# Attention with two chains of exponentiated scores: who adds the softmax denominators' parts, and five score banks in the last block

## The reference

```
x = x + attention(q = layernorm(x), kv = ctx)       # 16 heads of 32, 3202 keys, mask: key <= query
x = x + ffn(layernorm(x))                           # a mixture of 8 experts between two projections

scores = (q @ Wq.T + bq) . (kv @ Wk.T + bk) * 32**-0.5
attn   = softmax(where(key <= query, scores, -inf))
out    = (attn . (kv @ Wv.T + bv)) @ Wo.T + bo
```

## Time and profile before

| | us |
|---|---|
| median of three runs | 2900.06 |
| profiled execution, its own time | 2903.43 |
| its span, first to last instruction | 2901.8 |
| attention, about | 268 to 2051 |
| TensorE busy, share of the span | 2803.8, 97% |
| VectorE | 1873.2, 65% |
| GpSimd | 1570.4, 54% |
| ScalarE | 1521.4, 52% |

### The profile page before, as it was taken

One profiled execution on the slowest core, in us unless ns is written; L12 is line 12 of the kernel. 1 busy time (PEld: TensorE's weight loads), 2 busy tenths in 40 slices (PEclk: granted clock), 3 DMA queues, 4 the chain that ended last, 5 costly groups with the idle time before them and its releaser, 6 DMA issues. The chain is left out here.

```text
span 2901.8 us, 42115 instructions
## 1 busy us (share of the span) xinstructions
PE 2803.8 (97%) x15464; PEld 1655.4 (57%) x15464; DVE 1873.2 (65%) x3483; ACT 1521.4 (52%) x2904; POOL 1570.4 (54%) x717
## 2 busy tenths in 40 slices
PE   8989999999999999999999999999889999999996
PEld 7877555555555555555554555553576666655653
DVE  4367888886688876778876788860663544344544
ACT  3232456666566667566666566666334343444332
POOL 0000377888678888677888678888661210111110
PEclk9998899999999999999999999999999999999998
DMA  6568456668746778756778656677693110011000
GB/s 243 188 195 245 127 143 152 152 154 186 176 134 157 160 161 190 182 138 153 159 162 193 161 146 139 146 165 193 194 315 117 44 34 26 30 44 44 30 29 15
DMA packets 138708, 407.89 MB, mean 141 GB/s; under 512 B 11632, under 2 KB 28528, under 8 KB 111888
## 3 DMA queue, kind: packets, MB, share of 16 engines
q0 software_dynamic: 32272, 226.77, 33.2%
q1 hardware_dynamic: 101056, 169.07, 20.3%
q10 hardware_dynamic: 5184, 9.44, 1.0%
HBM read 114.33 MB, written 70.78 MB: 64 GB/s over the span
## 5 line engine op out<-in xcount | busy, mean ns | idle before, releaser
L1063 DVE TENSOR_REDUCE row_max<-m_bank 128x1 f32<-128x512 f32 (+4 forms) x2240 | 1254.1, 624 | 269.1 <-PE m_bank L1168 171.5
L1046 ACT ACTIVATE pT<-s_bank 128x512 f32<-128x512 f32 (+5 forms) x2176 | 1085.6, 578 | 621.6 <-PE s_bank L1213 444.6
L986 POOL TENSOR_TENSOR part_sum<-part_sum,pT 128x2048 f32<-128x2048 f32 (+1 forms) x252 | 1032.7, 4098 | 159.0 <-ACT pT L1046 150.8
L1213 PE MATMUL s_bank<-q_sb,k_sb 104*128 104x512 f32 (+3 forms) x2176 | 841.0, 411 | 12.6 <-ACT pT L1046 7.5
L1168 PE MATMUL m_bank<-k_sb,q_sb 96*128 96x512 f32 (+4 forms) x2240 | 843.9, 410 | 8.7 <-DVE den L1090 3.1
L1168 PEld LDWEIGHTS m_bank<-k_sb,q_sb 96*128 96x128 f32 x2240 | 432.3, 196 | 209.3 <-DVE row_max L1063 127.2
L1213 PEld LDWEIGHTS s_bank<-q_sb,k_sb 104*128 104x128 f32 x2176 | 411.5, 192 | 215.4 <-ACT pT L1046 124.4
L1230 PE MATMUL o_bank<-pT,v_sb 128*32 128x512 f32 (+5 forms) x4352 | 497.3, 574 | 0.0
L1639 POOL TENSOR_TENSOR f_var_eps<-f_mean_var,eps 128x4 f32<-128x4 f32 x8 | 1.6, 202 | 474.0 <-DVE f_mean_var L1858 474.0
L1230 PEld LDWEIGHTS o_bank<-pT,v_sb 128*32 128x32 f32 (+1 forms) x4352 | 113.3, 109 | 229.2 <-ACT pT L1046 112.2
L986 POOL TENSOR_TENSOR part_sum<-pT 128x2048 f32<-128x2048 f32 x28 | 127.8, 4565 | 134.9 <-ACT pT L1046 134.9
(11 more groups left out here) (198 smaller groups left out, 3378.4 us busy)
## 6 DMA issues: line engine op xcount, KB each, us to landing
moved_sum<-pT POOLq DMA_DIRECT2D x208, 1024.0 KB, 7.3
q_sb<-qT_hi SPq DMA_DIRECT2D x64, 256.0 KB, 5.1
k_sb<-kT_hi SPq DMA_DIRECT2D x48, 256.0 KB, 9.5
x_in<-in_x SPq DMA_DIRECT2D x8, 1024.0 KB, 6.1
qT_hi<-q_hi SPq DMA_DIRECT2D x8, 1024.0 KB, 4.2
qT_lo<-q_lo SPq DMA_DIRECT2D x8, 1024.0 KB, 6.5
q_sb<-qT_lo SPq DMA_DIRECT2D x32, 256.0 KB, 4.7
aT<-o_sb ACTq DMA_DIRECT2D x32, 256.0 KB, 5.3
```

Of the source, the lines that this page charges most:

```text
L986: pool.tensor_tensor(total, pT[:, slot(S - 1), :, q0:] if j and kt == 1 else total, pT[:, slot(S), :, q0:], ALU.add).then_inc(pool_added, 1)
L1046: act.activation(pT[0:rows, slot(S), h, q0:], s_bank[(HG * S + h) % S_RING][0:rows, q0:], ACT.Exp, scale=SCALE).then_inc(exp_done, 1)
L1063: dve.tensor_reduce(row_max[:, j % 2, r, h, c:c + 1], m_bank[p % M_BANKS][:, 0:n], AX_X, ALU.max).then_inc(unit_max, 1)
L1213: mm = pe.matmul(out[:, q0:], k_sb[0:R_END, h, at:at + P], q_sb[query_buffer(g, j)][0:R_END, h, q0:], start=True, stop=kt < 4 * j)
```

## The change

It has four parts.

1. In blocks 1 to 6 of each group, VectorE adds both chains into GpSimd's part (`fold`, two additions of 128 x 2048 values, float32, both inputs in SBUF). It does so one step into the next block (`FOLD_AFTER` = 1), behind the maxima of that step. TensorE then sums `part_sum` alone. There are 24 such blocks, so 48 additions.
2. The denominators of these blocks stand four steps into the next block in place of two (`DEN_AFTER`). The first moves of the next block's chains wait for the fold in place of the denominators.
3. In the last block five banks hold scores in place of three, two of `m_bank` joining the ring.
4. In the last block VectorE adds from key tile 4 on in place of 18 (`LAST_ADDS`). `STORE` goes from 7 to 6.

The planner learns of these: a fold costs VectorE 2.35 us in its list, the denominators cost TensorE less, and the last block's scores wait for a bank five back. So the whole order of units changes with it.

```diff
-LAST_ADDS = 18
+LAST_ADDS = 4
...
-DEN_AFTER, INVERT, SPREAD, NORMALISE, STORE = 2, 1, 2, 3, 7
-SUMS_BEHIND = {ST * g + FIRST_STEP[j + 1] + DEN_AFTER: (g, j) for g in range(NG) for j in range(QB) if (g, j) != (NG - 1, QB - 1)}
+DEN_AFTER, INVERT, SPREAD, NORMALISE, STORE = 4, 1, 2, 3, 6
+SUMS_BEHIND = {ST * g + FIRST_STEP[j + 1] + (DEN_AFTER if 0 < j < QB - 1 else 2): (g, j)
+               for g in range(NG) for j in range(QB) if (g, j) != (NG - 1, QB - 1)}
+FOLD_AFTER = 1
+def folded_chains(g, j):
+    if j in (0, QB - 1):
+        return ()
+    return range(CHAINS) if j >= 1 else range(1)
...
+T_FOLD = 2.35
+LAST_SCORE = HG * (len(ALL_STEPS) - key_tiles(QB - 1))
+def score_before(n):
+    if n < LAST_SCORE + S_RING:
+        return n - S_RING
+    return n - LAST_RING if n >= LAST_SCORE + LAST_RING else None
...
+        if h == HG - 1 and S in FOLDS_AT:
+            x = x._replace(dve=max(x.dve, end) + T_FOLD * len(folded_chains(*FOLDS_AT[S])))
...
-                        reach(pool, block_done, QB * g + (j if j > 1 else 0))
+                        if (*previous_chains(g, j), c) in FOLD_NUMBER:
+                            reach(pool, folded, FOLD_NUMBER[(*previous_chains(g, j), c)])
+                        else:
+                            reach(pool, block_done, QB * g + (j if j > 1 else 0))
...
+                def fold(g, j):
+                    reach(dve, pool_added, PO * g + PO_BEFORE[FIRST_STEP[j + 1]])
+                    for c in folded_chains(g, j):
+                        reach(dve, moved[c], 16 * (TR[c] * g + TR_BEFORE[c][FIRST_STEP[j + 1]]))
+                        reach(dve, folded, FOLD_NUMBER[g, j, c] - 1)
+                        dve.tensor_tensor(part_sum[:, j % 2], part_sum[:, j % 2], moved_sum[:, c], ALU.add).then_inc(folded, 1)
...
-                    for c in range(CHAINS) if j else ():
+                    chains = [c for c in range(CHAINS) if j and c not in folded_chains(g, j)]
+                    for c in chains:
...
+                    if folded_chains(g, j):
+                        reach(pe, folded, FOLD_NUMBER[g, j, folded_chains(g, j)[-1]])
...
-                    out = s_bank[n % S_RING]
+                    out = score_bank(n)
```

More of the change, by code:

```diff
@@ L456 @@
 S_RING, M_BANKS = 3, 4
+LAST_RING = S_RING + 2
 def key_tiles(j):
@@ L536, with previous_chains @@
 TR = [TR_BEFORE[c][ST] for c in range(CHAINS)]
-DEN_AFTER, INVERT, SPREAD, NORMALISE, STORE = 2, 1, 2, 3, 7
-SUMS_BEHIND = {ST * g + FIRST_STEP[j + 1] + DEN_AFTER: (g, j) for g in range(NG) for j in range(QB) if (g, j) != (NG - 1, QB - 1)}
+DEN_AFTER, INVERT, SPREAD, NORMALISE, STORE = 4, 1, 2, 3, 6
[6 more added lines that the diff above has]
+    return range(CHAINS) if j >= 1 else range(1)
+FOLDS = [(g, j, c) for g in range(NG) for j in range(QB) for c in folded_chains(g, j)]
+FOLD_NUMBER = {fold: n + 1 for n, fold in enumerate(FOLDS)}
+FOLDS_AT = {ST * g + FIRST_STEP[j + 1] + FOLD_AFTER: (g, j) for g, j, _ in FOLDS}
+def previous_chains(g, j):
+    return (g, j - 1) if j > 1 else (g - 1, QB - 1)
 def max_units(j):
@@ L670, in sums_time @@
             return 0
-        j = SUMS_BEHIND[2 * v][1]
+        g, j = SUMS_BEHIND[2 * v]
         own = sum(widths(j, kt) for kt in range(key_tiles(j)) if adder(j, kt) == "matmul")
-        return T_VALUES * (1 + (CHAINS if j else 0) + own) + T_TURN
+        return T_VALUES * (1 + (CHAINS - len(folded_chains(g, j)) if j else 0) + own) + T_TURN
     def slot_free(self, x, S):
@@ L704, in score @@
         turn, behind = self.turned(x)
-        pe = max(x.pe, x.exp_end[0] + T_TO_WRITE) + turn + self.score_time(j, kt)
+        before = score_before(x.n)
+        pe = max(x.pe, x.exp_end[before - x.n] + T_TO_WRITE if before is not None else 0) + turn + self.score_time(j, kt)
         act = max(x.act, pe + T_TO_READ) + 0.06 + (T_EXP - 0.06) * widths(j, kt)
         end, copied = act + T_EXP_END - T_EXP, x.copied
+        if h == HG - 1 and S in FOLDS_AT:
+            x = x._replace(dve=max(x.dve, end) + T_FOLD * len(folded_chains(*FOLDS_AT[S])))
         if x.n + 1 == x.copied_by:
@@ L756, in best @@
     def best(self):
-        kept = [State(0, 0, 0, "scores", 9, 0, 0, 0, (0,) * S_RING, (), (0,) * M_BANKS, 0, 0, 0, None)]
+        kept = [State(0, 0, 0, "scores", 9, 0, 0, 0, (0,) * LAST_RING, (), (0,) * M_BANKS, 0, 0, 0, None)]
         for _ in range(self.scores + self.pairs + len(self.left)):
@@ L862, in attend @@
         p_used = t.sem("p_used")
+        folded = t.sem("chains_folded")
         pool_added, moved = t.sem("pool_added"), [t.sem(f"moved_sum_added{c}") for c in range(CHAINS)]
@@ L866, in attend, with score_bank @@
         TILES = HG * ST
+        def score_bank(n):
+            if n < LAST_SCORE:
+                return s_bank[n % S_RING]
+            k = (n - LAST_SCORE) % LAST_RING
+            return s_bank[(LAST_SCORE + k) % S_RING] if k < S_RING else m_bank[(len(BANK_JOBS) - S_RING + k) % M_BANKS]
         def slot(S):
@@ L1045, in _ @@
                         reach(act, s_done, HG * S + h + 1)
-                        act.activation(pT[0:rows, slot(S), h, q0:], s_bank[(HG * S + h) % S_RING][0:rows, q0:],
+                        act.activation(pT[0:rows, slot(S), h, q0:], score_bank(HG * S + h)[0:rows, q0:],
                                        ACT.Exp, scale=SCALE).then_inc(exp_done, 1)
@@ L1122, in _ @@
                         spread(*SUMS_AT[S - SPREAD])
+                    if S in FOLDS_AT:
+                        fold(*FOLDS_AT[S])
                     if vector_adds(g, j, kt):
@@ L1209, in scores @@
                     n = HG * S + h
-                    reach(pe, exp_done, max(0, n - S_RING + 1))
-                    out = s_bank[n % S_RING]
+                    before = score_before(n)
+                    if before is None:
+                        bank_free(len(BANK_JOBS) - S_RING + n - LAST_SCORE)
+                    else:
+                        reach(pe, exp_done, max(0, before + 1))
+                    out = score_bank(n)
                     at = key_column(g, kt)
```

4 lines of the change are left out of this document (2 added, 2 removed).

## The result

| | median, us | runs, us | profiled span, us | mean clock |
|---|---|---|---|---|
| before | 2901.4 | 4: 2897.0 to 2902.9 | 2901.8 | 0.979 |
| after | 2981.2 | 4: 2977.3 to 2997.2 | 2977.9 | 0.965 |

The ratio is 1.028, with an interval of 1.026 to 1.030: slower by 80 us. The forecast was 2915, its range ended at 2938. The sign was right, the size was not.

A forecast was written before the change was run, and what follows sets the result against it. TensorE was taken to set attention's pace, with VectorE also near its limit. The terms - 26 - 5 + 52 - 5 + 9 - 10 = +15 us on a median of 2900.1 gave 2915 us, range 2872 to 2938.

The forecast's parts named there:

- chains' matmuls gone, sparse pairs, piles: In attention: TensorE's saved matmuls with ones, -26 and -5 us; fewer step pairs without units, -5; piled units in group 0, +9.
- TensorE waits for the folds: At the denominators of blocks 1 to 5: 46 us of waits plus 6 where four units stand ahead, 52 us in all.
- last block: Moves leave earlier, with the DMA as the next limit: gain 10 us, bounds 18 and 4.
- So the two engines take turns: VectorE's folds and GpSimd's 4.57 us addition, both reading SBUF, exclude each other for a whole instruction; folds end at 901.3.
- The step that failed: At the denominators behind the folds: TensorE can do nothing else and waits 2.3 us, 20 times, 46 us.
- Its own upper bound: For the folds: VectorE's whole 3.5 us of waiting and part of its 4.6 us of work on TensorE's path, 100 us.
- The third rival: In dense blocks VectorE becomes the bound, maxima, folds and waiting together exceeding TensorE's work: 2945 us; chance 0.14.
- The piles: In group 0, units pushed to the step where they fall due, 23, 22 and 18 in three pairs: cost 9 us.
- Pairs of 5.2 us: In the last block each pair of steps brings a 1.05 MB move, so pairs go from 5.5 to 5.2 us.
- The first rival: VectorE's folds are not held by GpSimd and the 52 us go: 2863, up to 2880 where half are held; chance 0.30.

The follow-up runs named there:

- run 9: The changed kernel with folds that add only 8 of each tile's 512 queries, the order of every engine kept: 2880.2 us, ratio 0.993.
- run 5: The changed kernel with ten useless matmuls ahead of TensorE's wait, only at the 11 places where it waits for the fold alone: 2963.2 us, ratio 1.021.
- run 3: The changed kernel with GpSimd's first addition of blocks 2 to 7 done over 8 of 512 queries, the folds whole: 2879.8 us, ratio 0.9915.
- run 7: The changed kernel with one chain folded, at step 0 of the next block where GpSimd is idle, and denominators at 2 steps: 2877.9 us, ratio 0.991.
- run 1: The changed kernel with only its last block's part: no folds, denominators two steps behind in every block: 2895.8 us, ratio 0.9975.
- run 2: The changed kernel with the last block's three score banks and VectorE's additions from key tile 18 restored, folds kept: 2991.2 us, ratio 1.031.

## Why the prediction was right in sign and wrong in size

The account on the profiled executions, 76 us (2977.9 - 2901.8). A block's time is that between two copies of its output on ScalarE. Two terms are read from the traces as they are, the waits and the last block. The clock is half of a count of low clock, and the first row is not measured: it is what the other three leave of 76.

| term | predicted | found |
|---|---|---|
| chains' matmuls gone, sparse pairs, piles: -31 - 5 + 9 | -27 | -24 (the rest) |
| TensorE waits for the folds | +52 | +61 |
| last block | -10 | -10 |
| TensorE's clock | none | +49 (half of 99 us) |
| sum | +15 | +76 |

*The folds.* "So the two engines take turns" held at 4.57 us as at 1.3, which no row of before showed. Moved to the new place (GpSimd's start there is 37.9 us later), the prediction had GpSimd done at 935.0, the folds at 939.2 and TensorE ready at 936.9; the trace has 935.0, 939.5 and 937.1. The Trainium skill's "SBUF — State Buffer", section "SBUF: two separate sides", has the port pair held for the whole instruction; run 9's 0.19 us addition that takes 4.47 us agrees. The term itself was too small by 9: the 20 waits of blocks 1 to 5 came to 56 us (about 2.5 each, 3.06 where a fourth unit stands ahead), and blocks 6 of groups 0 to 2, which I costed at nothing, waited 2.47, 1.23 and 1.12 us.

*The step that failed* is "TensorE waits 2.3 us. 20 times that is 46 us": a wait was priced at its own length. The prediction noted the upper clock level ahead of the change and had no term for it behind. In the blocks behind block 0 of group 0 the clock was low for 105.5 us in the changed kernel and for 17 in the one before; in the 100 us behind attention for 17 and 6.8. Half of the difference is 49 us (the later stages, with 47 and 44, are left out). Of the 105.5, 72 stand behind 13 of the 23 waits, so 61 us of waiting cost about 36 more; 20 stand behind the two large piles. That low clock costs about half its length can be read where the same block ran with and without it. Block 1 of group 1, which neither fold nor pile touches, in the kernels before, after, and of run 9:

```profile
768.31:799.34 31.03, 29.62 (x196) 16.26 (x194) 20.78 (x44) 15.90 (x35) 18.55 (x8) 0.89 0.36 112
```
```profile
802.75:832.12 29.37, 28.40 (x194) 15.34 (x193) 19.62 (x42) 15.71 (x34) 18.35 (x8) 0.94 0.40 123
```
```profile
777.10:804.84 27.74, 26.75 (x194) 14.79 (x193) 19.60 (x42) 15.61 (x34) 18.33 (x8) 1.00 0.50 143
```

31.0 us with 6.8 us of low clock, 29.4 with 3.4, 27.7 with none: 0.48 us for each. So the kernel before was itself slowed there by a fall, and a difference of one block between two kernels need not come from its code. Run 5's blocks gave 0.4; at that price the clock's term is 39 and the first row -14. By half, runs 3 and 9, which have no such waits, leave -29 and -26 in the first row, near the change's -24. Undoing the turns (run 3) took away 61 us of waits and 67 of low clock in the blocks (38 are left of 105.5), 34 at half: 95 of the 101 us. The prediction's term for the folds was 52. Its own upper bound was 100, and the range had left that out: 2915 + 48 = 2963 should have been its end. The third rival's own 2945 lay outside it too. Even 2963 is 18 us short.

*The third rival* (VectorE becomes the bound) falls as the account of the 101 us. In run 3 VectorE does all of its 110 us of folding and the kernel is faster than before. And the weight loads for units, which wait for VectorE's maxima, waited 144.9 us in the changed kernel and 144.8 in run 3: what the turns added does not stand at the units. It was 127.2 before the change, so the units do wait longer for VectorE in both; what that costs no run shows.

*The piles.* I said 9 us of TensorE waiting. They cost about 13 in blocks 2 and 3 of group 0, and once more it is the clock. Block 2 of group 0 in run 9 (a pile of 23 units) and in run 7 (18):

```profile
351.21:401.03 49.82, 48.47 (x254) 25.87 (x253) 42.44 (x74) 24.11 (x51) 29.47 (x12) 0.86 0.46 123
```
```profile
350.49:393.77 43.28, 42.37 (x261) 23.63 (x260) 40.19 (x73) 24.04 (x52) 29.49 (x12) 1.00 0.54 141
```

6.5 us more at 0.86: 13.7 us of low clock, half of which is 6.8. Elsewhere the order gives and takes: in run 9, blocks 2 to 4 of groups 1 to 3 are 25 us shorter than before, blocks 5 and 6, where the units go, 9 us longer.

*The last block.* In the profile it is 11.8 us shorter, and 3.4 us less of low clock make 1.7 of that, which leaves 10. It gained 7.4 alone (run 1) and lost 10 when undone (run 2). "Pairs of 5.2 us" were 5.14, the DMA share near 1. What I had not seen is that the first pairs run ahead at 4.44 us and the rest then wait; and TensorE's last denominators wait 4.1 us for the last move:

```profile
2119.07 3.64 PE L1247 MATMUL m_bank<-moved_sum,ones 128*32 128x512 f32 x16 [4.10 <-DMA moved_sum<-pT]
```

*The first rival* (folds not held) is not what this kernel does. Run 3 made it so that no fold was held and took 2880, 17 us above the rival's 2863; its upper end of 2880 was meant for half of them held, so the agreement is luck.

Open: what of the remaining 17 us (the first row of the table, against 41 us of matmuls gone) is idle time at ScalarE's rhythm and what is full blocks. Why the clock fell behind 13 of the waits and not behind ten others of much the same length was not tried.

## What to carry to other kernels

A move of work from a full engine to one with room is priced by whom the new work meets, instruction by instruction: here 2.3 us beside a GpSimd addition of 4.57 us became 5.7 to 6.5 in 24 cases, and in GpSimd's gap of 3.2 us it stayed 2.3 and TensorE did not wait. Price a new wait of TensorE above its length (here some 1.6 times), and look at the granted clock behind it, since TensorE counts as busy while it runs at half speed. Where two costs share one slack, as the turn and the fold's own time did, removing either takes away the whole loss; only removing each alone tells that neither by itself is its cause.

## What the runs showed of the hardware that was not expected

- VectorE's addition with two inputs in SBUF waits until a GpSimd addition that is under way has ended, whatever its own size: 0.19 us of work took up to 4.47 us (run 9), 2.28 took up to 6.48.
- Behind 13 of 23 waits of TensorE of 1.1 to 3.4 us its clock was granted at the lower level for 3.4 to 10.2 us, 72 in all, with TensorE shown as busy for 85% or more of each; behind the other ten it was not. The same happened in the two large piles, 10.2 us in each, where TensorE pauses for 0.7 us ahead of it.
- 2.35 us of useless matmuls in such a wait, at 11 places, made the kernel 18 us faster (run 5).
- Moves with addition of 1 MB inside SBUF, issued faster than they land, came 5.14 us apart at 205 to 222 GB/s and a DMA share of 1.02 to 1.04.
